# A four-layer gated cross-attention block: scores two heads ahead of their exponentials, and another order for VectorE in the first program

## The reference

```python
q = (queries @ Wq + bq).reshape(b, sq, 16, 8).transpose(0, 2, 1, 3)
k, v = ...
scores = jnp.einsum('bhqd,bhkd->bhqk', q, k) * scale
probs = jax.nn.softmax(jnp.where(mask, scores, neg), axis=-1)
out = jnp.einsum('bhqk,bhkd->bhqd', probs, v).reshape(b, sq, 128) @ Wo + bo
x = x + jnp.tanh(g) * out
```

## Time and profile before

| | |
|---|---|
| median of 3 runs | 1021.7 us (1021.55 to 1022.72) |
| the profiled execution | 1020.51 us |
| its span | 1018.7 us |
| TensorE, matmul | 882.3 us busy, 87% |
| VectorE | 685.1 us, 67% |
| ScalarE | 470.4 us, 46% |
| GpSimd | 119.3 us, 12% |
| mean granted TensorE clock | 0.97 of 2.4 GHz |

### The profile page before, as it was taken

One profiled execution on the slowest core, in us unless ns is written; L12 is line 12 of the kernel. 1 busy time (PEld: TensorE's weight loads), 2 busy tenths in 40 slices (PEclk: granted clock), 3 DMA queues, 4 the chain that ended last, 5 costly groups with the idle time before them and its releaser, 6 DMA issues.

```text
span 1018.7 us, 14302 instructions
## 1 busy us (share of the span) xinstructions
PE 882.3 (87%) x4731; PEld 598.6 (59%) x4731; DVE 685.1 (67%) x2069; ACT 470.4 (46%) x1134; POOL 119.3 (12%) x206
## 2 busy tenths in 40 slices
PE   2698999968778689789999999999999988899966
PEld 1355545433435566666667676767666766677744
DVE  3845726392866967967668678768766777877734
ACT  0376565677586565565353442443253232322312
POOL 3000100040221301300001001001000111100112
PEclk9999999988899999989999999999999999999989
DMA  6800000000000000000000000000000000000000
GB/s 174 249 1 2 1 1 1 1 0 1 1 1 1 1 1 1 1 2 1 1 1 2 1 1 1 1 1 2 1 1 1 1 1 11 1 11 1 2 10 11
DMA packets 12063, 12.70 MB, mean 12 GB/s; under 512 B 3758, under 2 KB 7896, under 8 KB 11992
## 3 DMA queue, kind: packets, MB, share of 16 engines
q1 hardware_dynamic: 9272, 9.98, 3.2%
q10 hardware_dynamic: 2336, 1.29, 0.5%
q0 software_dynamic: 384, 0.53, 0.2%
HBM read 10.75 MB, written 1.05 MB: 12 GB/s over the span
## 4 chain that ended last, share of the span: by engine, by line
PE 59%; DVE 24%; ACT 7%; issue 5%; POOL 2%; ACTq 0%; POOLq 0%; DVEq 0%
PE bank L1680 10%; PE bank L1668 6%; PE bank L1588 5%; PE bank L1670 5%; PE bank L1669 5%; DVE nm L1188 3%; PE bank L1473 3%; PE bank L1601 3%; DVE hb L1332 3%; DVE hb L1323 2%; DVE x L1312 2%; PE bank L1726 2%; PE bank L1426 2%; PE bank L1651 2%; PE bank L1645 2%
## 5 line engine op out<-in xcount | busy, mean ns | idle before, releaser
L1000 ACT ACTIVATE hb<-bank 96x512 f32<-96x512 f32 (+1 forms) x160 | 95.1, 594 | 203.1 <-PE bank L1670 202.5
L1680 PEld LDWEIGHTS bank<-m_w,hb 128*128 128x128 f32 (+1 forms) x1280 | 166.1, 195 | 23.1 <-issue 5.5
L1668 PE MATMUL bank<-parts,m_w_lo 128*96 128x512 f32 (+1 forms) x320 | 152.1, 475 | 31.4 <-DVE hb L1323 22.7
L1680 PE MATMUL bank<-m_w,hb 128*128 128x128 f32 (+1 forms) x1280 | 175.6, 281 | 2.3 <-DVE hb L1323 2.1
L1332 DVE SCALAR_TENSOR_TENSOR hb<-hb,bank 96x512 f32<-96x512 f32 (+1 forms) x160 | 109.1, 682 | 96.2 <-ACT hb L1000 95.4
L1670 PE MATMUL bank<-parts,m_w_hi 128*96 128x512 f32 (+1 forms) x320 | 127.3, 398 | 0.0
L1669 PE MATMUL bank<-parts,m_w_hi 128*96 128x512 f32 (+1 forms) x320 | 127.1, 397 | 0.0
L1323 DVE TENSOR_TENSOR hb<-hb,bank 96x512 f32<-96x512 f32 (+1 forms) x160 | 109.8, 686 | 10.5 <-PE bank L1670 5.0
L1668 PEld LDWEIGHTS bank<-parts,m_w_lo 128*96 128x96 f32 (+1 forms) x320 | 59.0, 184 | 78.9 <-DVE hb L1323 34.6
L1601 PE MATMUL bank<-Qs,KT 112*77 112x512 f32 x192 | 88.7, 501 | 2.7 <-DVE invt L1238 1.4
L1485 PE MATMUL bank<-KT,Qs 96*128 96x308 f32 x192 | 77.2, 424 | 13.2 <-ACT PTs L909 7.1
(11 more groups left out here) (271 smaller groups left out, 1482.0 us busy)
## 6 DMA issues: line engine op xcount, KB each, us to landing
m_w_raw<-in_L_ffn_w_dram SPq DMA_DIRECT2D x2, 1024.0 KB, 6.6
m_w<-in_L_ffn_W_dram SPq DMA_DIRECT2D x1, 1408.0 KB, 9.5
x<-in_x_dram ACTq DMA_DIRECT2D x4, 256.0 KB, 6.6
out_dram<-x SPq DMA_DIRECT2D x4, 256.0 KB, 2.0
f_out<-in_L_ffn_Wout_dram POOLq DMA_DIRECT2D x8, 64.0 KB, 3.3
m_w_raw<-in_L_ffn_W_experts_dram SPq DMA_DIRECT2D x1, 512.0 KB, 10.5
ctxn<-in_ctx_dram ACTq DMA_DIRECT2D x4, 38.5 KB
Wq<-in_L_xattn_Wq_dram SPq DMA_DIRECT2D x2, 64.0 KB
```

Of the source, the lines that this page charges most:

```text
L1000: act.activation(hb[n % 3][0:m, :], bank[UP[u, n]][0:m, :], ACT.Tanh, scale=0.5).then_inc(*chunk_act.up(u, n))
L1668: pe.matmul(dst, w_lo, x_hi, start=True, stop=False)
L1680: op = pe.matmul(bank[7][:, t * P:(t + 1) * P], hb[n % 3][0:m, t * P:(t + 1) * P], wd, start=i == 0 and t == 0, stop=ends_expert(k, n) and ...
```

## The change

In the body of an attention with heads, TensorE computes the scores of heads 0, 1 and 2 at head 0, and at head h those of head h + 2. The number of banks (three), their assignment (h % 3) and all other orders stay.

In the first program VectorE multiplies f0_out and makes the mask rows right after its own copies, then the factor copies, the fold of bo, f0_in, f0_bias and t_w1b. TensorE does the matmuls for bo first and signals them by themselves ("bo"), then t_w1's, and waits for the load group "side" only ahead of the f0_wout matmul, which carries the signal "columns".

```diff
@@ the first program, VectorE
-                for i in range(len(groups)):
-                    dve.wait_ge(*kept(i))
-                dve.wait_ge(*landed["small"].at("all"))
-                for l in range(3):
-                    for wide, w in ((WqR, Wq), (WkR, Wk)):
...
-                dve.tensor_copy(f0_in[:].rearrange("p (m i) -> p m i", i=I0), nat_in[:].unsqueeze(2).to_broadcast([P, M0, I0]))
+                dve.wait_ge(*kept(2))
                 dve.wait_ge(*landed["f0"].at("all"))
                 for c in range(C0):
                     dve.tensor_scalar(f0_out[:, c, :], f0_out[:, c, :], f0_cols[:, 2, c:c + 1], None, ALU.mult)
-                dve.wait_ge(*turned.at("columns"))
-                dve.tensor_tensor(f0_bias[:], bank[0][:, 0:1], f0_bout[:], ALU.add)
-                dve.tensor_tensor(bo_f[:].rearrange("o l n -> o (l n)"), bank[2][0:2, 0:3 * P], bo_f[:].rearrange("o l n -> o (l n)"), ALU.add) \
...
                 dve.wait_ge(*landed["rows"].at("all"))
...
+                for i in range(len(groups)):
+                    dve.wait_ge(*kept(i))
+                dve.wait_ge(*landed["small"].at("all"))
+                for l in range(3):
+                    for wide, w in ((WqR, Wq), (WkR, Wk)):
...
+                dve.wait_ge(*turned.at("bo"))
+                dve.tensor_tensor(bo_f[:].rearrange("o l n -> o (l n)"), bank[2][0:2, 0:3 * P], bo_f[:].rearrange("o l n -> o (l n)"), ALU.add) \
...
+                dve.tensor_copy(f0_in[:].rearrange("p (m i) -> p m i", i=I0), nat_in[:].unsqueeze(2).to_broadcast([P, M0, I0]))
+                dve.wait_ge(*turned.at("columns"))
+                dve.tensor_tensor(f0_bias[:], bank[0][:, 0:1], f0_bout[:], ALU.add)
                 for f, s in enumerate((ROOT / (N * S2), -ROOT / N, 1.0 / (N * (S2 - 1)))):
                     dve.tensor_scalar(t_w1b[:, f, :], bank[1][:, f * 64:(f + 1) * 64], s, None, ALU.mult)
@@ the first program, TensorE
                 for i in range(len(groups)):
                     pe.wait_ge(*kept(i))
-                for name in ("small", "side"):
-                    pe.wait_ge(*landed[name].at("all"))
-                pe.matmul(bank[0][:, 0:1], f0_wout[:], f0_b2[:], start=True, stop=True)
+                pe.wait_ge(*landed["small"].at("all"))
                 for l in range(3):
-                    pe.matmul(bank[2][0:2, l * P:(l + 1) * P], bv[:, l:l + 1].to_broadcast([P, 2]), Wo[l][:], start=True, stop=True)
+                    op = pe.matmul(bank[2][0:2, l * P:(l + 1) * P], bv[:, l:l + 1].to_broadcast([P, 2]), Wo[l][:], start=True, stop=True)
+                op.then_inc(*turned.up("bo"))
                 for f in range(3):
-                    op = pe.matmul(bank[1][:, f * 64:(f + 1) * 64], ident[0:3, f:f + 1].to_broadcast([3, P]), t_w1T[:], start=True, stop=True)
-                op.then_inc(*turned.up("columns"))
+                    pe.matmul(bank[1][:, f * 64:(f + 1) * 64], ident[0:3, f:f + 1].to_broadcast([3, P]), t_w1T[:], start=True, stop=True)
+                pe.wait_ge(*landed["side"].at("all"))
+                pe.matmul(bank[0][:, 0:1], f0_wout[:], f0_b2[:], start=True, stop=True).then_inc(*turned.up("columns"))
@@ the second program, TensorE, body
                     scores(0)
+                    scores(1)
                     for h in range(H):
-                        if h + 1 < H:
-                            scores(h + 1)
+                        if h + 2 < H:
+                            scores(h + 2)
                         if h % J == 0 and h:
                             weigh(h // J - 1)
```

More of the change, by code:

```diff
@@ L421, in _ @@
                         op.then_inc(*keptD.up(i))
-                for i in range(len(groups)):
-                    dve.wait_ge(*kept(i))
-                dve.wait_ge(*landed["small"].at("all"))
-                for l in range(3):
-                    for wide, w in ((WqR, Wq), (WkR, Wk)):
-                        dve.tensor_copy(wide[l][:].rearrange("p g (q c) -> p g q c", c=32),
-                                        w[l][:].rearrange("p (g c) -> p g c", c=32).unsqueeze(2).to_broadcast([P, G, QK // 32, 32]))
-                dve.tensor_copy(f0_in[:].rearrange("p (m i) -> p m i", i=I0), nat_in[:].unsqueeze(2).to_broadcast([P, M0, I0]))
+                dve.wait_ge(*kept(2))
                 dve.wait_ge(*landed["f0"].at("all"))
@@ L463, in _ @@
                     .then_inc(*masks_ready.up("all"))
+                for i in range(len(groups)):
[3 more added lines that the diff above has]
+                    for wide, w in ((WqR, Wq), (WkR, Wk)):
+                        dve.tensor_copy(wide[l][:].rearrange("p g (q c) -> p g q c", c=32),
+                                        w[l][:].rearrange("p (g c) -> p g c", c=32).unsqueeze(2).to_broadcast([P, G, QK // 32, 32]))
+                dve.wait_ge(*turned.at("bo"))
+                dve.tensor_tensor(bo_f[:].rearrange("o l n -> o (l n)"), bank[2][0:2, 0:3 * P], bo_f[:].rearrange("o l n -> o (l n)"), ALU.add) \
+                    .then_inc(*folded.up("bo_whole"))
+                dve.wait_ge(*folded.at("bo_whole"))
+                dve.tensor_copy(bo_p[:, 0].bitcast(F32R), bo_f[:]).then_inc(*folded.up("bo_high"))
+                dve.wait_ge(*folded.at("bo_high"))
+                dve.tensor_tensor(bo_p[:, 1], bo_f[:], bo_p[:, 0], ALU.subtract).then_inc(*folded.up("bo_rest"))
+                dve.wait_ge(*folded.at("bo_rest"))
+                dve.tensor_scalar(bo_p[:, 0], bo_p[:, 0], ident[0:2, 0:1], None, ALU.mult).then_inc(*folded.up("bo_low"))
+                dve.wait_ge(*folded.at("bo_low"))
+                dve.scalar_tensor_tensor(out=bo[:], in0=bo_p[:, 1], scalar=ident[0:2, 1:2], in1=bo_p[:, 0],
+                                         op0=ALU.mult, op1=ALU.add)
+                dve.tensor_copy(f0_in[:].rearrange("p (m i) -> p m i", i=I0), nat_in[:].unsqueeze(2).to_broadcast([P, M0, I0]))
+                dve.wait_ge(*turned.at("columns"))
+                dve.tensor_tensor(f0_bias[:], bank[0][:, 0:1], f0_bout[:], ALU.add)
                 for f, s in enumerate((ROOT / (N * S2), -ROOT / N, 1.0 / (N * (S2 - 1)))):
```

## The result

The new kernel takes **1028.3 us** in the median (1025.5 to 1028.8) against 1022.2 of the kernel before (1021.6 to 1022.7) in the same comparison: a ratio of 1.0058, interval 1.0041 to 1.0074. It is slower by about 6 us. The forecast was 1022.6, and the range went up to 1026.6; the measured time is 5.7 us above the first and 1.7 above the second. The profiled execution took 1025.5, the lowest of the four, with a span of 1023.5.

A forecast was written before the change was run, and what follows sets the result against it. It took two VectorE idle stretches (5.7 and 2.7 us) in the first program as on the path, and TensorE and ScalarE as awaiting each other in A5. -5.4 + 6.3 = +0.9 on 1021.7 gave 1022.6, range 1016.3 to 1026.6.

The forecast's parts named there:

- Part 1: First program: VectorE's new order fills idle time; the second program starts at 24.1 in place of 29.57, minus 5.4 us.
- the landing of the mask rows: First program: their loads land at 17.0 us, bounds 16.5 and 18.26; the gain is 5.7 or 4.3 at the bounds.
- m1_w1, the second program's first need: Start of the second program: load lands at 24.8, first conversion at 25.0, covered by 0.2 us; nothing charged.
- Part 2: Attention units with heads: scores two ahead make TensorE wait for exponentials; plus 6.3 us, ends about 2 and 10.
- A0 and A1: Layer 0's first two attention units, beside weight preparation: weighings of four heads each (W) start later; 1.1 each, 2.2 us.
- A6 and A7: Layer 1's last two units: wait at the start, another at head 8's scores (S(8)) mostly swallowed; 0.6 each, 1.2 us.
- A2 and A3: Layer 0's last two units, TensorE saturated: one score more done before the first weighing; minus 0.4 us together.
- A4, A5 and A8 to A11: Layer 1's first two units, TensorE and ScalarE awaiting each other: 1.9 us; layer 2's first two 1.4, last two 0.
- the ring spreads: Rival, all twelve units with heads: 0.38 us for each of three weighings, 14 us, giving 1030.3; chance 0.17.
- the first program doesn't end earlier: Rival, first program: something unseen holds it or m1_w1 comes late; 1021.7 + 6.3 = 1028; chance 0.04.
- Nearly free: Rival, units with heads: other tracks' slack takes up the waits, loss below 3.4 us; 1016.3 with no loss; chance 0.35.
- The clock rival: Rival, A0, A1 or A5: more short TensorE waits bring one slow clock stretch costing 3 us, giving 1025.6; chance 0.08.

The follow-up runs named there:

- rows_early: order_only with the ten mask-row loads moved ahead of x and ctx on ScalarE's queue; 1014.3 us, ratio 0.9918.
- lead_l2: The kernel before, with scores two heads ahead in layer 2 (A8 to A11) alone; 1026.0 us, ratio 1.0037.
- order_only: The changed kernel's new first program, with scores one head ahead as in the kernel before; 1019.5 us, ratio 0.9971.
- factors_first: order_only with the factor copies ahead of the mask rows' steps in the first program; 1017.5 us, ratio 0.9955.
- lead_l1: The kernel before, with scores two heads ahead in layer 1 (A4 to A7) alone; 1024.6 us, ratio 1.0034.
- lead_behind: Scores two heads ahead, but issued behind the weighing and the turn of that step, against the kernel before; 1025.0 us, ratio 1.0027.
- lead_only: The kernel before with its old first program, and scores two heads ahead in all units; 1031.3 us, ratio 1.0083.
- lead_a67: The kernel before, with scores two heads ahead in A6 and A7 alone; 1026.4 us, ratio 1.0041.

## Why the prediction was wrong, step by step

- **Part 1, the order of the work.** Right: multiplies at 12.74, TensorE's bo matmuls done at 19.7, f0_wout before VectorE needs it, the factors through to the end without a gap. **Failed: the landing of the mask rows**, "I take 17.0", with 18.26 as the upper bound. They landed at 19.64. The lower bound held but was not near, and the upper one was none: the queue's last packets had indeed passed by 17.0 in the new kernel too, and the signal that the loads were complete was there only 2.6 us later; and the landing of a group on another queue says nothing of how late this one can be. The step was worth 5.4 and gave 3.0. This was also one of the prediction's own signs of being wrong ("if mask rows land past 18.3").
- The Trainium skill (DMA: Bandwidth & Descriptors, Queues, rings and completion order) says that a transfer's increment of its semaphore lands only after all earlier writes of the same DMA engine, whichever queue they came by. SyncE's queue still moved small packets past 19.5 us, so this could account for the 2.6 us, and for the rows' quick landing when they are issued early. No run here parts it from a plain delay of the signal; why the rows land so late stays open, and what rows_early shows is only that an earlier issue brings them earlier.
- **m1_w1, the second program's first need**, cost nothing, as charged; in rows_early, where the second program starts another 4.7 us earlier, ScalarE's first conversion does wait for it, and this delays nothing that counts (VectorE's normalized x begins at 25.22 in place of 29.93, again 4.7 earlier):

```profile
24.58 0.63 ACT L841 ACTIVATE m_w_hi<-m_w_raw 128x512 fp32r<-128x512 f32 x1 [1.78 <-DMA m_w_raw<-in_L_ffn_w_dram]
```

- **Part 2, A0 and A1: mis-sized**, 2.2 forecast, 3.2 measured. W(0) +0.47, W(1) +0.94, W(2) +1.77 in A0 are the 0.45, 0.8, 1.5 of the text. What failed is "W(3) 1.1, since its turn of outputs has no S ahead of it". W(3) follows W(2) at 3.2 us in both kernels (16.19 - 12.99, 17.94 - 14.76), so nothing came back.
- **A6 and A7: failed**, 1.2 forecast, 3.1 by the W. The step is "a second wait at S(8), mostly swallowed because W(1) waits 1.25 us for VectorE's att anyway". That wait was not slack but the end of a loop through the delayed scores themselves. The upper end of its range, 1.6, was nearly the value for each (1.52 and 1.54).
- **A2 and A3: wrong sign, small**: -0.4 forecast, +0.2 by the W. ScalarE's spared waits were worth nothing there.
- **A4, A5 and A8 to A11: right in kind.** A4 and A5: 1.9 forecast, 1.8 at equal clock, but 1.3 by the medians with an interval that holds 0. A8 and A9: 1.4 forecast, 1.2 by the W, with the gap at the start of A8 (0.73 us, 0.8 foretold); A10: 0 by the W, as forecast. The runs of lead_l2 give more than the W for this layer, 2.3 to 3.9, and what the rest is stays open.
- Sum of the lead: 6.3 forecast, 8.7 to 10 measured. Of the excess, 1.9 us lie in A6 and A7, 1.0 in A0 and A1, 0.6 in A2 and A3, by the W. Together with the 2.4 us that Part 1 fell short this makes about the difference of 5.7. The rival "the ring spreads" gave 1030.3 and named A6 to A9 as the place from which it would decide; in mechanism it came closest, though A8 to A11 did not pay at each group. The number nearest to 1028.3 is the 1028 of "the first program doesn't end earlier", by luck: that program did end 3.0 us earlier, and the lead cost more than the 6.3 that this figure has in it. "Nearly free" failed because in TensorE's order no other track's work stands between a waiting score and its W.
- **The clock rival: failed.** The clock over all runs is no lower with the lead (0.969, before 0.966), and A0's heads stay at 1.00 after the change, with waits of up to 0.65 us in them. Around the start of A5's heads slow stretches come with the lead and without it (from 290 to 300, 3.1 us lost after, 3.4 in order_only, 0.8 before). A halved stretch at the start of A0's heads does occur, in order_only, factors_first, lead_l1 and lead_behind; it makes W(0) 0.65 us later, and none of the four has scores two ahead in front of W there, so it isn't the lead's. The Trainium skill (TensorE: Matmul & The Clock Gate, A second HAM failure mode) lets a clock swing where TensorE idles briefly between groups of matmuls as it cycles through banks. The traces do show a clock that swings, before as well as after; that more such waits make it swing more they don't show (30.9 us lost before, 30.8 after). The slow stretch ahead of A10 came in the traces of after, lead_only, lead_behind, lead_l2, but also in lead_l1 and lead_a67, which have no lead in A8 and A9, and in none of the other eight; what decides where such a stretch falls stays open.

## What to carry to other kernels

Before an instruction that may wait is moved ahead in an engine's order, list what stands behind it: a producer that runs further ahead pays for each wait with everything queued behind it, and a wait further down absorbs it only if what feeds that wait doesn't itself stand behind the moved one. A load that nobody waits for has no visible landing; its last packet isn't one, and the first reader should be placed late, or the load issued early, rather than counted on. And where run times follow a clock that wanders, compare at equal clock, or by distances between instructions, before a layer is blamed.

## What the runs showed that was not expected

- Ten small loads (5 KB in all) moved ahead of the 1.2 MB of x and ctx on one queue cost the latter nothing that the traces show (x lands 4.2 us behind its issue in place of 6.8), and brought 4.6 us against order_only at equal clock; "small", on the other queue, came at least 1.0 us earlier along with them than in the earliest other trace (16.60 for 17.65).
- The mask rows' signal came 2.6 us after their queue's last packet was counted (19.64, 17.0).
- From run to run of the unchanged kernel the mean granted clock lies between 0.958 and 0.976, and with it the time spreads over 12 us (1016.6 to 1028.6), more than the whole change is worth.
- Halved stretches of TensorE's clock stand at different places in traces whose instructions there are the same or nearly so: at the start of A0's heads in four of fourteen, ahead of A10 in six.
